# Seeding the first steps of a chunk: two graph-attention layers in one kernel

## The reference

```
layer 0: scores[i,j] = s[i] + t[j]      s = (x @ W) @ a1, t = (E @ W) @ a2
         att = softmax_j(where(adj > 0, leaky(scores, 0.2), -9e15))
         x = layernorm(x + elu(att @ E + x))
layer 1: wh = x @ W1; scores[i,j] = s[i] + t[j] from wh, slope 0.01, same adj
         x = layernorm(x + att @ wh + bias)
```

## Time and profile before

| | |
|---|---|
| median of 3 runs | 660.71 us (660.51 to 661.35) |
| the profiled execution | 661.77 us |
| its span | 660.0 us |
| VectorE busy | 575.0 us, 87% |
| ScalarE busy | 516.2 us, 78% |
| TensorE matmul busy | 515.8 us, 78% |
| seeds (L605) / VectorE's steps (L816) | 184 / 136 |

### The profile page before, as it was taken

The page is one execution under the profiler, slowest core; times in us unless marked ns, Lnnn a source line. Parts: engine busy times, 40 slices in busy tenths (PEclk is TensorE's granted clock), DMA queues, the critical chain, the costliest instruction groups (busy, mean ns, idle before and its releaser), DMA issues.

```text
span 660.0 us, 14220 instructions
## 1 busy us (share of the span) xinstructions
PE 515.8 (78%) x6038; PEld 230.8 (35%) x6039; DVE 575.0 (87%) x729; ACT 516.2 (78%) x592; POOL 191.6 (29%) x143
## 2 busy tenths in 40 slices
PE   1304779899989799999988318778897898899894
PEld 1202345343443344444454203233333233333341
DVE  3888998999999898888467889989998998899685
ACT  0855998899999996898676227979997899699673
POOL 0110000388028850672083000004311450232240
PEclk9999889899999899999998758999999999999998
DMA  7899885687478727430200000000000001000000
GB/s 165 319 360 334 280 285 210 241 288 257 180 242 291 250 94 287 132 126 2 73 3 18 1 32 1 1 33 1 2 9 33 1 1 33 1 1 18 1 17 9
DMA packets 18631, 76.46 MB, mean 116 GB/s; under 512 B 6552, under 2 KB 8776, under 8 KB 10376
## 3 DMA queue, kind: packets, MB, share of 16 engines
q1 hardware_dynamic: 17560, 74.63, 32.5%
q0 software_dynamic: 256, 0.80, 0.4%
q10 hardware_dynamic: 752, 0.13, 0.1%
HBM read 74.47 MB, written 1.09 MB: 114 GB/s over the span
## 4 chain that ended last, share of the span: by engine, by line
PE 31%; DVE 25%; ACT 20%; issue 14%; DMA 4%; POOL 3%; SPq 1%; POOLq 0%; ACTq 0%; DVEq 0%
PE acc L941 16%; ACT Pm L613 14%; DVE junk L722 12%; PE zps L986 9%; DVE zps L816 8%; PE acc L948 4%; DMA adj_in<-in_adj 4%; ACT zps L605 2%; ACT v L506 2%; SPq L350 1%; DVE v L701 1%; DVE tAB L697 1%; ACT u_row L522 1%; DVE tot L757 0%; DVE tot L753 0%
## 5 line engine op out<-in xcount | busy, mean ns | idle before, releaser
L613 ACT ACTIVATE Pm<-zps,ebias 128x1024 f32<-128x1024 f32 (+1 forms) x320 | 293.4, 933 | 82.6 <-DVE zps L816 68.3
L722 DVE CUSTOM_DVE_ANT_0 junk<-v,u_row 128x2048 int8<-128x2048 int8 (+3 forms) x136 | 304.6, 2261 | 2.0 <-ACT v L506 1.8
L986 PE MATMUL zps<-D,v 128*128 128x128 bf16 x2048 | 173.7, 224 | 56.1 <-DVE D L744 29.1
L986 PEld LDWEIGHTS zps<-D,v 128*128 128x128 fp8e4 x2048 | 118.7, 99 | 216.3 <-issue 87.3
L816 DVE SCALAR_TENSOR_TENSOR zps<-S_row,tau_col,zps 128x1024 f32<-128x1024 f32 (+1 forms) x136 | 142.0, 1050 | 50.6 <-PE zps L986 47.7
L605 ACT ACTIVATE zps<-S_row,ntau_col 128x1024 f32<-128x1024 f32 (+1 forms) x184 | 176.6, 960 | 5.4
L941 PE MATMUL acc<-Pm,X 128*32 128x512 f32 (+1 forms) x1280 | 145.5, 527 | 20.2 <-ACT Pm L613 17.8
L941 PE MATMUL acc<-Pm,VE 128*32 128x512 f32 (+1 forms) x1280 | 148.6, 538 | 8.5 <-ACT Pm L613 3.9
L398 POOL TENSOR_TENSOR tAB<-flag,totW 128x520 f32<-128x520 f32 (+1 forms) x8 | 10.3, 1287 | 282.5 <-issue 138.7
L948 PE MATMUL acc<-Pm,ones 128*32 128x256 f32 (+1 forms) x1280 | 87.8, 347 | 0.0
L948 PEld LDWEIGHTS acc<-Pm,ones 128*32 128x32 f32 x1280 | 43.1, 115 | 72.2 <-issue 62.7
(11 more groups left out here) (147 smaller groups left out, 286.4 us busy)
## 6 DMA issues: line engine op xcount, KB each, us to landing
adj_in<-in_adj SPq DMA_DIRECT2D x64, 1024.0 KB, 5.6
S_row<-S_rows_scratch SPq DMA_DIRECT2D x5, 512.0 KB, 3.7
S_row<-S_rows_scratch SPq DMA_DIRECT2D x3, 256.0 KB, 3.1
u_row<-u_row_scratch SPq DMA_DIRECT2D x3, 256.0 KB, 3.5
out<-tAB SPq DMA_DIRECT2D x3, 256.0 KB, 2.6
S_row<-S_rows_scratch POOLq DMA_DIRECT2D x1, 512.0 KB, 11.1
S_row<-S_rows_scratch POOLq DMA_DIRECT2D x1, 256.0 KB, 8.0
out<-tAB SPq DMA_DIRECT2D x2, 128.0 KB, 2.0
```

The costliest lines, as they stand in the source:

```text
L613: a.activation(Pm[:, k % PB, 0:R(C) * P], zps[:, buf("step", k), 0:R(C) * P], ACT.Exp, bias=ebias[:, int(seeded(k)), J:J + 1])\
L722: d.tensor_tensor_reduce(out=junk[:, at % 2, 0:cols.stop - cols.start], in0=v_bytes[:, rt, cols], in1=u_row[:, cols], scale=1.0, scalar=-3 ...
L986: last = t.matmul(zps[:, buf("step", k), r * P:(r + 1) * P], v[:, chunks[C][1] + r, J * P:(J + 1) * P], D[:, C % 2, r, :], start=(r * P % ...
```

## The change

A step may be seeded where the user three places before it in the buffer is a step. Before, that had to be a step of the same chunk, so the first steps of a chunk, whose buffers were last used by the chunk before, could not be seeded. Now it may be a step of an earlier chunk of the same layer that is at least as wide. The seed is then issued while the older chunk still runs, reads the other S_row buffer, and waits until that row has landed. The second edit picks, out of the steps that may be seeded, as many as before in number but with another formula: of each interval the first step and not the last. SEEDS is unchanged.

```diff
@@ seeded_steps
             may = [k for k in range(JT * C, JT * (C + 1)) if place["step", k] >= ZB
-                   and users[place["step", k] - ZB][0] == "step" and users[place["step", k] - ZB][1] >= JT * C]
+                   and users[place["step", k] - ZB][0] == "step"
+                   and users[place["step", k] - ZB][1] >= JT * FIRSTS[layer(C)]
+                   and R(users[place["step", k] - ZB][1] // JT) >= R(C)]
             n = SEEDS[layer(C)][C - FIRSTS[layer(C)]]
-            seeded_steps |= {k for i, k in enumerate(may) if (i + 1) * n // len(may) > i * n // len(may)}
+            seeded_steps |= {k for i, k in enumerate(may) if i * n % len(may) < n}
@@ scalar
                     for n in seeds_at.get(k, []):
+                        of = n // JT
+                        if of > C:
+                            wait_S(act, of)
                         wait_buf(act, "step", n)
-                        a.activation(zps[:, buf("step", n), 0:R(C) * P], S_row[:, C % 2, 0:R(C) * P], ACT.Relu,
+                        a.activation(zps[:, buf("step", n), 0:R(of) * P], S_row[:, of % 2, 0:R(of) * P], ACT.Relu,
                                      bias=ntau_col[:, n % JT:n % JT + 1]).then_inc(seed_done, 1)
```

## The result

The changed kernel takes 666.85 us (median of 4 runs, 666.42 to 667.23), against 661.03 us for the kernel before beside it: a ratio of 1.0083, with a 95% interval from 1.0063 to 1.0104. That is 5.5 us more by the ratio (4.2 to 6.9 by its interval), where the forecast had +2.8. The profiled span grew from 660.0 to 665.4 us.

The account below looks back on a forecast made before the run. Bounds differ by chunk: ScalarE and VectorE in 2, TensorE in 3, though VectorE is busy 87% overall. Terms 1.3 + 0.4 - 0.8 + 1.1 + 1.3 - 0.5 = +2.8 us: 660.71 becomes 663.5, range 662.1 to 665.8.

Parts of the forecast that it names:

- Step 30 ahead of the diagonals: Ends of chunks 3 and 6: VectorE's unseeded step 30 delays the next chunk's first turn, +0.4 and 1.2 us.
- The end of chunk 4: Unseeded step 31 delays the four row maxima and the layer's epilogue on VectorE: +1.1 us, bounds 0.7 to 1.3.
- the end of chunk 8: Unseeded step 31 comes behind the diagonals, so TensorE's product 31 is late: +0.7 us.
- The main reason: At chunk borders, product 31 and `save_acc` order what follows, not exp 0, so borders stay as long as before.
- the sentence on chunk 3: Inside chunk 3 TensorE is the bound, so nothing VectorE or ScalarE saves there counts; no time term.
- Chunk 2: Chunk 1 to 2: early seeds delay `save_acc` 1.0 us, step 17 adds 0.3: +1.3 us, bounds -0.5 to +2.3.
- Chunk 4: Seeded step 3 spares VectorE a narrow step ahead of `save_o` and GpSimd's chain: -0.8 us, bounds -1.1 to 0.
- Chunk 7 behind turn 5: Rest of chunk 7 with the border to chunk 8: more VectorE steps, partly absorbed by idle time, +1.6 us.
- Chunks 6 and 7 together: Late first turn of chunk 7, early gain and later VectorE steps inside it: +1.3 us, bounds -0.2 to +2.3.
- That the border wait goes and stays gone: Chunks 2, 3, 4, 7, 8: exp 0 is spared VectorE's step, together -5.9 us, giving 654.8; chance 0.22.
- That VectorE's total counts: Whole kernel: VectorE's total counts, not the order; one step fewer, -1.28 us, giving 659.4; chance 0.07.
- Contention as the rival had it: Moved chains meet four more row maxima, 0.85 us longer each: 3.4 us on top, giving 666.9; chance 0.08.

Follow-up runs that it names:

- the run with the ends put back: Changed kernel with step 30 seeded for 29 in chunks 3, 6, 7, 31 for 30 in chunk 4, 31 added in chunk 8: 666.03 us.
- The one-seed runs: Changed kernel with one seed moved per chunk: 19 for 18 in chunks 3 and 6, 666.88 us; 15 for 14 in chunk 8, 667.32 us.
- the pair of runs named there: Two edits of the changed kernel that differ in chunk 6 only by step 19 seeded for 18: 666.03 and 661.43 us.
- the rule by which chunk 7 gains 3.4: Kernel before with only the first edit, seeds allowed across the border, and the old formula picking the last step of each interval: 664.58 us.
- The version with chunks 6 and 7 redone: Kernel before with a new set of 18 seeds in chunk 7 and the same pattern, started at 3 and 4, in chunk 6: 657.93 us.
- the kernel with chunk 2 put back: Changed kernel with chunk 2's old set, steps 0 and 2 unseeded and step 17 seeded: 668.27 us.

## Where the prediction was right, and where it failed

**Direction and mechanism at the borders: right.** `save_acc` of chunk 1 was to start near 185.3 and started at 185.53. VectorE's sums of chunk 2 were to be 1 us late and are 1.2 to 1.3. Step 30 ahead of the diagonals was to cost 0.4 and 1.2 us and cost 0.3 and 1.3; the run with the ends put back returned 0.3 and 1.0. The end of chunk 4 has its +1.1, the end of chunk 8 its +0.7, TensorE's gap of 2.2 us in chunk 8 is gone for -1.2. The main reason, that exp 0 doesn't set a border's length, is confirmed twice: by the four borders whose way from turn 0 to `save_acc` is the same to 0.01 us, and by the added seeds of step 0, which left two of these ways as they were and made two 0.4 us longer, and shortened one chunk by 0.3 us.

**The step that failed** is the sentence on chunk 3: TensorE works 64.39 of 65.1 us, "so nothing that VectorE or ScalarE saves inside it counts". The sentence is about savings and was used for losses as well: the inside of chunk 3, and of chunk 8 beyond its gap ("TensorE, the bound from there, keeps it"), got no term. A chunk whose bound is TensorE gains next to nothing from VectorE's side, but can be made longer, as soon as VectorE's other work between two of its steps outlasts the seeded steps there. The busy share of 99% said only that the set of before nearly avoided this. Chunk 6 got no term either, and for it the sentence doesn't even hold: in the kernel before VectorE works 56.9 of its 59.4 us and TensorE 51.0. The prediction shows no row of it and names only its first moved seed, step 3 for 4, of ten. The two edits together move 8 of the 16 seeds of chunk 3, 10 of the 18 of chunk 6 and 5 of the 10 of chunk 8, and nothing in the formula knows where the row maxima and conversions stand. That is +2.0, +1.3 (some 0.8 of it the slow stretch) and +1.9 us without a term.

The one-seed runs give back 1.4 of the 2.0 and 1.2 of the 1.9 us at the places named, and the pair of runs named there 0.6 of chunk 6. In chunk 8, 0.8 of the 1.2 is the order alone; in chunk 3 the row maximum is also 1.0 us shorter once it is out of GpSimd's way. Two other places of the same look hold the rest: in chunk 3 near 284, where ScalarE idles 2.20 us, some 0.9 us, against 0.3 gained at turn 4, and in chunk 8 between turns 11 and 12 0.7. They weren't tried one by one.

**Terms that were off in size.** Chunk 2: +0.7 and not +1.3; the save is 0.8 late against its own turn, and the last 0.3, step 17 ahead of a sum, never reached the chunk's end. Chunk 4: -1.5 and not -0.8, but 1.2 of it is the slow stretch that the kernel before has at 354 to 357 and the kernel after doesn't; the seeded step 3 itself gave 0.4, by turn 5. Chunk 7 behind turn 5: forecast +1.6, measured -0.1. The border to chunk 8 costs 1.5, and 1.6 are gained between turns 5 and 31, of which the prediction had nothing: TensorE's gap of 2.39 us at turn 14 is gone, and the chunk's row maxima take 37.5 us and not 39.7, since fewer of them meet GpSimd's chain. Of the 1.6, 0.3 is the slow stretch of before. Chunks 6 and 7 together came to +1.1, against +1.3 forecast. That agreement is luck: a missing loss (+1.3 in chunk 6) and a missing gain (1.6 in chunk 7) cancel. Without the slow stretches the sum would be some 0.7 us further from the forecast (an estimate: 5.5 + 1.2 + 0.3 - 0.8 = 6.2).

**The rivals.** That the border wait goes and stays gone is refuted. That VectorE's total counts is refuted most plainly: VectorE works 2.4 us less and the kernel is 5.5 slower, and the five added seeds of step 0 take VectorE to 569.8 us, 5.2 less than before, with a loss. Contention as the rival had it, with four more row maxima 0.85 us longer, was wrong in its sum and right in its kind: over the whole kernel the row maxima take 306.5 us after and 307.5 before. By chunks it does move time, 1.1 us more row maximum in chunk 3 (3.27 us at 298.12, where 2.28 is usual), 0.6 more in chunk 8, 2.2 less in chunk 7. Its number, 666.9, is near the result for another reason.

**Open.** How much of a total difference of 1 us between two of these kernels is queue and how much slow clock can't be settled, for the reason in the last section. The shares of order and contention in chunks 3 and 7 weren't separated; no run has the one without the other. Why chunk 8 loses 5.0 us by the rule by which chunk 7 gains 3.4 was read only at their gaps, and not tested.

## What to carry to other kernels

An engine with in-order work of two kinds (here: steps that others wait for, and row maxima and conversions that nobody waits for soon) needs its relief where the other work stands, not evenly spread: walk through its queue between each two awaited instructions, add up what stands there, and compare it with the consumer's pace times the steps covered in between. A chunk where the consumer is 99% busy is one in which this sum fits nearly everywhere; an edit that moves the pattern deserves a loss term there and at most a small gain. Look also at what the moved work then runs beside: a row maximum cost 2.28 us or 3.3 us here, by its place against GpSimd's chain. And in a small edit of a schedule, read its effect in the stretch where it was made, with a fixed event as the ruler; the total of the kernel can move by as much for another reason.

## What the hardware showed

TensorE's slow stretches come and go in places that weren't edited. In chunk 8 the kernel before has a gap of 2.22 us and no slow stretch behind it; the next turn takes 0.62 us (timeline of TensorE):

```profile
576.90 0.62 PE L986 MATMUL zps<-D,v 128*128 128x128 bf16 x8
```

The kernel with step 0 seeded on top of before has the same gap at the same place, and this behind it:

```profile
575.27 1.07 PE L946 MATMUL acc<-Pm,X 128*32 128x512 f32 x8 [2.22 <-ACT Pm L618]
576.27 1.02 PE L991 MATMUL zps<-D,v 128*128 128x128 bf16 x8
577.23 1.94 PE L946 MATMUL acc<-Pm,X 128*32 128x512 f32 x8
```

A turn takes 1.02 in place of 0.62 us and a product 1.94 in place of 1.06, the lower of the two clock levels (1.2 in place of 2.4 GHz; the granted clock from 576.27 to 579.20 is 0.51) for some 3 us, and the chunk is 1.5 us longer for it by turn 10, and still at its end. The version with chunks 6 and 7 redone has it at the same place. Likewise near 513 in chunk 7, behind a gap of 1.92 us that is the same in all of them: none in the kernel after, but one in the kernel with chunk 2 put back and in the one with chunk 8's seed moved, 1.5 us each, and in the one with a seed of chunks 3 and 6 moved, 1.2 us. Gaps of 1.4 to 2.5 us are followed by it in some of the profiled executions and not in others. What a slow stretch costs its chunk depends on who sets the pace behind it: 0.8 to 1.5 us in chunks 4, 6 and 8 and behind turn 5 of chunk 7, and 0.3 us behind turn 14 of chunk 7, where VectorE does. The Trainium skill (TensorE: Matmul & The Clock Gate, Part 1: The HAM clock gate) says that the monitor behind the clock runs on its own and doesn't start with the kernel, so that the place of a change of clock differs from run to run; the rows above fit it, and no run here tests it by itself. What follows for reading: differences of a whole time of 1 us between kernels that both have such gaps aren't evidence on an edit, and what removes a gap of 2 us can be worth 3.
